# A six-sublayer decoder on one core: the order of matrix products in self-attention, the output projections in cross-attention, and eight-bit products with three weight tables

## The reference

```python
# 1 (cross-attention, 2, has the same skeleton with norms, rotation and a mask)
q = q * cq + rotate_half(q) * cq;  k = k * ck + rotate_half(k) * ck
attn = softmax(einsum('bhnd,bhmd->bhnm', q, k) * scale)
out  = einsum('bhnm,bhmd->bhnd', attn, v).reshape(b, n, H * HD) @ Wo
# 6
q1 = (input1 * scale).astype(float8_e4m3fn);  q2 = (input2 * scale1).astype(float8_e4m3fn)
out = (q1.astype(float32) / scale) @ (q2.astype(float32) / scale1)
```

## Time and profile before

| what | value |
|---|---|
| three executions | 2940.96, 2946.80, 2949.22 us, median 2946.8 us |
| the profiled execution | 2954.18 us, of which the span is 2952.3 us |
| TensorE busy | 2691.4 us, 91% of the span |
| VectorE busy | 1891.6 us, 64% |
| ScalarE busy | 1323.2 us, 45% |
| GpSimd busy | 1256.0 us, 43% |
| mean granted TensorE clock | 0.953 |

### The profile page before, as it was taken

One profiled execution on the slowest core, in us unless ns is written; L12 is line 12 of the kernel. 1 busy time (PEld: TensorE's weight loads), 2 busy tenths in 40 slices (PEclk: granted clock), 3 DMA queues, 4 the chain that ended last, 5 costly groups with the idle time before them and its releaser, 6 DMA issues. The chain is left out here.

```text
span 2952.3 us, 65025 instructions
## 1 busy us (share of the span) xinstructions
PE 2691.4 (91%) x23700; PEld 2323.1 (79%) x23700; DVE 1891.6 (64%) x4030; ACT 1323.2 (45%) x3154; POOL 1256.0 (43%) x1605
## 2 busy tenths in 40 slices
PE   6999999996699999999999979996999999699985
PEld 5888888886588888888888868885777777477773
DVE  5555555554677777777777744444777777366657
ACT  2222222222566666666666633332433333266656
POOL 3111111111476767676767601113455454334434
PEclk9999999998899999999999989997999999799985
DMA  4000000001100000000000020000000000000001
GB/s 141 7 7 4 7 7 4 6 4 41 58 6 5 4 5 4 5 4 5 4 5 4 2 74 0 0 0 28 13 8 11 7 11 0 26 30 28 28 4 58
DMA packets 42505, 49.12 MB, mean 17 GB/s; under 512 B 4032, under 2 KB 33600, under 8 KB 41920
## 3 DMA queue, kind: packets, MB, share of 16 engines
q1 hardware_dynamic: 42432, 48.16, 5.0%
HBM read 35.56 MB, written 4.19 MB: 13 GB/s over the span
## 5 line engine op out<-in xcount | busy, mean ns | idle before, releaser
L1033 ACT ACTIVATE b_probs<-bank,b_shift,b_q_scale 128x128 f32<-128x128 f32 x512 | 228.4, 462 | 0.6
L1092 POOL TENSOR_TENSOR b_rows<-b_rows,b_swapped 128x512 f32<-128x512 f32 x160 | 204.5, 1287 | 56.2 <-DVE b_swapped L878 56.2
L518 POOL TENSOR_TENSOR a_probs<-a_probs,a_rs 128x512 f32<-128x512 f32 x64 | 66.8, 1043 | 311.1 <-DVE a_rs L414 303.9
L1139 POOL TENSOR_TENSOR b_probs<-b_probs,b_rs 128x512 f32<-128x512 f32 x128 | 133.2, 1040 | 136.6 <-DVE b_rs L930 133.5
L2583 ACT ACTIVATE d_probs<-d_probs 128x512 f32<-128x512 f32 x128 | 78.9, 630 | 240.6 <-DVE d_probs L2482 238.7
L46 PE MATMUL bank<-a_xT,a_wq 128*128 128x256 f32 x512 | 153.7, 300 | 26.6 <-DVE a_xT L381 26.6
L1102 POOL TENSOR_TENSOR b_rms<-b_rms,sh_minus_half 128x8 f32<-128x8 f32 (+1 forms) x128 | 169.6, 1325 | 10.7
L886 DVE TENSOR_REDUCE b_ss<-b_squares 128x4 f32<-128x512 f32 x192 | 125.2, 680 | 73.7 <-ACT b_squares L1008 73.7
L134 POOL TENSOR_SCALAR sh_rstd<-sh_meanvar 128x2 f32<-128x2 f32 (+1 forms) x80 | 17.7, 222 | 326.0 <-DVE sh_meanvar L120 264.1
L46 PE MATMUL bank<-b_wo,b_oT 128*128 128x256 f32 x512 | 149.9, 293 | 1.4 <-DVE b_oT L852 1.4
L389 DVE TENSOR_TENSOR a_qT<-bank,a_cos 128x256 f32<-128x256 f32 x256 | 95.3, 419 | 85.2 <-PE bank L48 85.2
(11 more groups left out here) (350 smaller groups left out, 9060.0 us busy)
## 6 DMA issues: line engine op xcount, KB each, us to landing
a_xT_in<-in_xT SPq DMA_DIRECT2D x16, 256.0 KB, 2.6
sh_x<-in_x SPq DMA_DIRECT2D x1, 4096.0 KB, 25.0
b_ctx_in<-in_ctxT SPq DMA_DIRECT2D x32, 128.0 KB, 2.0
d_x_in<-sh_x SPq DMA_DIRECT2D x16, 256.0 KB, 2.3
e_x_in<-sh_x SPq DMA_DIRECT2D x16, 256.0 KB, 2.4
e_cT<-in_ctxT SPq DMA_DIRECT2D x32, 128.0 KB, 2.5
out<-sh_x SPq DMA_DIRECT2D x16, 256.0 KB, 2.1
a_qT<-in_L_attn_Wq SPq DMA_DIRECT2D x1, 2048.0 KB, 8.5
```

The source lines that it names most:

```text
L1033: op = act.activation(probs[:, g % 2, keys], bS[:, keys], ACT.Exp, bias=shift[:, g % 2, a:a + 1], scale=q_scale[:, g, a // 2, a % 2:a % 2 ...
L1092: pool.tensor_tensor(rows[:, unit, :], rows[:, unit, :], swapped[:, half, :], ALU.add).then_inc(added[unit], 1)
L1139: pool.tensor_tensor(pr, pr, rs[:, g % 2, :].unsqueeze(2).to_broadcast([128, R, 128]), ALU.mult).then_inc(probs_ready[g], 1)
```

## The change

In self-attention the attention of a group runs later against the projections and a third turn, `older`, comes in. TensorE's order becomes: s0 p2' q0 | s1 t0 q1 p3' | s2 t1 w0 q2 p0 | s3 t2 w1 q3 p1 | t3 w2 k w3 v v, where p2' and p3' belong to the turn before `before`. The islands are s0; s1 t0; s2 t1 w0; s3 t2 w1; t3 w2; w3: six. VectorE starts its turn with `low_o(older, 3)` and `low_x(now)`, takes the older turn's residual after group 1 and its statistics after group 2; ScalarE takes `take_o` ahead of the next `exponent` and copies the next rows at the end of its turn; GpSimd normalises after group 2. In cross-attention `project_out(old, 2)` moves to just ahead of `project_out(old, 3)`. In the eight-bit block `over`, `under` and `excess` go; `inner` is `coarse` clamped, and with w twice and w times minus two, fine·w + coarse·2w − inner·2w takes the place of fine·w + excess·w: twelve products in a turn.

```diff
@@ self-attention, TensorE
-            def turn(now, before):
+            def turn(now, before, older):
                 if before is not None:
                     scores(before, 0)
+                if older is not None:
+                    project_out(older, G - 2)
                 if now is not None:
                     pe.wait_ge(x_low, nth(now, 1, 1))
                     q_proj(now, 0)
-                for g in range(1, G):
+                if before is not None:
+                    scores(before, 1)
+                    transpose_probs(before, 0)
+                if now is not None:
+                    q_proj(now, 1)
+                if older is not None:
+                    project_out(older, G - 1)
+                for g in range(2, G):
                     if before is not None:
                         scores(before, g)
                         transpose_probs(before, g - 1)
+                        weigh_values(before, g - 2)
                     if now is not None:
                         q_proj(now, g)
                     if before is not None:
-                        weigh_values(before, g - 1)
-                        if g >= 2:
-                            project_out(before, g - 2)
+                        project_out(before, g - 2)
+                if before is not None:
+                    transpose_probs(before, G - 1)
+                    weigh_values(before, G - 2)
                 if now is not None:
                     k_proj(now)
                 if before is not None:
-                    transpose_probs(before, G - 1)
+                    weigh_values(before, G - 1)
                 if now is not None:
                     v_proj(now, 0)
-                if before is not None:
-                    weigh_values(before, G - 1)
-                if now is not None:
                     v_proj(now, 1)
-                if before is not None:
-                    project_out(before, G - 2)
-                    project_out(before, G - 1)
@@ self-attention, VectorE
-            def turn(now, before, after):
-                if before is not None:
-                    maximum(before, 0)
-                    total(before, 0)
+            def turn(now, before, older):
+                if older is not None:
+                    low_o(older, G - 1)
                 if now is not None:
-                    take_q(now, before, 0)
-                for g in range(1, G):
+                    low_x(now)
+                for g in range(G):
                     if before is not None:
                         maximum(before, g)
+                        if g >= 2:
+                            low_o(before, g - 2)
+                        total(before, g)
                     if now is not None:
                         take_q(now, before, g)
-                    if before is not None:
-                        total(before, g)
-                        low_o(before, g - 1)
+                    if older is not None and g == 1:
+                        residual(dve, sh, older, 2, [b[:, 0:D] for b in bY], y_ready, res_ready, norm_done)
+                    if older is not None and g == 2:
+                        row_stats(dve, sh, older, 2, res_ready, stats_ready, meanvar_ready)
+                if before is not None:
+                    low_o(before, G - 2)
                 if now is not None:
                     take_k(now, 0)
                     take_k(now, 1)
-                if before is not None:
-                    low_o(before, G - 1)
-                if after is not None:
-                    low_x(after)
-                if before is not None:
-                    residual_stats(dve, sh, before, 2, [b[:, 0:D] for b in bY], y_ready, res_ready, stats_ready, meanvar_ready, norm_done)
@@ self-attention, ScalarE
                 if before is not None:
                     exponent(before, 0)
-                for g in range(1, G):
-                    if before is not None:
+                    take_pT(before, 0)
+                    exponent(before, 1)
+                    for g in range(2, G):
                         take_pT(before, g - 1)
+                        take_o(before, g - 2)
                         exponent(before, g)
-                        take_o(before, g - 1)
-                if before is not None:
                     take_pT(before, G - 1)
+                    take_o(before, G - 2)
                     take_o(before, G - 1)
@@ cross-attention, TensorE
             def turn(new, mid, old):
                 project_vc(mid)
-                project_out(old, 2)
                 turn_unit(mid, Q + 2)
                 scores(mid, 1)
                 turn_unit(mid, Q + 3)
+                project_out(old, 2)
                 project_out(old, 3)
@@ eight-bit block
-                    for k, part in enumerate((fine, excess)):
+                    for k, (part, by) in enumerate(((fine, w), (coarse, w_twice), (inner, w_away))):
...
             def scale_rows(i):
                 act.wait_ge(turned, i + 1)
-                free(act, over_ready, i)
+                free(act, y_ready, i)
                 act.activation(coarse[:, i % 2, :], bT[i % 2][:, :], ACT.Copy, scale=halves[:, 0:1], saturate=False).then_inc(coarse_ready, 1)
+                free(act, fine_ready, i)
...
-                dve.tensor_scalar(over[:, i % 2, :], coarse[:, i % 2, :], TOP, 2.0, ALU.max, ALU.mult).then_inc(over_ready, 1)
+                dve.tensor_scalar(inner[:, i % 2, :], coarse[:, i % 2, :], TOP, -TOP, ALU.min, ALU.max, saturate=False).then_inc(inner_ready, 1)
```

More of the change, by code:

```diff
@@ L438, in turn @@
                     take_k(now, 1)
-                if before is not None:
-                    low_o(before, G - 1)
-                if after is not None:
-                    low_x(after)
-                if before is not None:
-                    residual_stats(dve, sh, before, 2, [b[:, 0:D] for b in bY], y_ready, res_ready, stats_ready, meanvar_ready, norm_done)
[L446 to L451, removed]
+            turn(0, None, None)
+            turn(1, 0, None)
+            with dve.Fori(2, n_turns) as i:
+                turn(i, i - 1, i - 2)
+            turn(None, n_turns - 1, n_turns - 2)
+            turn(None, None, n_turns - 1)
         @block.scalar
@@ L484, in take_o, with turn @@
                     act.copy(of_batch(0, g, b), bO[b][:, :].rearrange("p (r h q) -> p r h q", r=2, h=R)).then_inc(o_taken, 1)
[L486 to L488 removed]
+            def turn(now, before, following):
                 if before is not None:
                     exponent(before, 0)
[L491 to L492 removed]
+                    take_pT(before, 0)
+                    exponent(before, 1)
+                    for g in range(2, G):
                         take_pT(before, g - 1)
+                        take_o(before, g - 2)
                         exponent(before, g)
[L495 to L496 removed]
                     take_pT(before, G - 1)
+                    take_o(before, G - 2)
                     take_o(before, G - 1)
@@ L501, in turn @@
                     take_v(now, 1)
[L503 to L506, removed]
+                if following is not None:
+                    high_x(following)
+            high_x(0)
+            turn(0, None, 1)
+            with act.Fori(1, n_turns - 1) as i:
+                turn(i, i - 1, i + 1)
+            turn(n_turns - 1, n_turns - 2, None)
+            turn(None, n_turns - 1, None)
         @block.gpsimd
@@ L513, in _, with turn @@
             pool.wait_ge(x_loaded, 16)
-            with pool.Fori(0, n_turns) as i:
+            def turn(now, before):
                 for g in range(G):
[L516 to L519, removed]
+                    if now is not None:
+                        pool.wait_ge(rs_ready, nth(now, G, g + 1))
+                        pr = probs[:, g % 2, :].rearrange("p (a k) -> p a k", k=S)
+                        pool.tensor_tensor(pr, pr, rs[:, g % 2, :].unsqueeze(2).to_broadcast([128, 8, S]), ALU.mult).then_inc(probs_ready, 1)
+                    if before is not None and g == 2:
+                        normalise(pool, sh, before, 2, meanvar_ready, norm_step, norm_done)
+            turn(0, None)
+            with pool.Fori(1, n_turns) as i:
+                turn(i, i - 1)
+            turn(None, n_turns - 1)
 def cross_attention_block(nc, sh):
@@ L1413, in fp8_matmul_block @@
         unscale = sb("unscale", [128, 1])
-        edge = sb("edge", [128, 1])
         scaled = sb("scaled", [128, 3, 512])
         coarse = sb("coarse", [128, 3, 512], FP8)
-        over = sb("over", [128, 3, 512], BF16)
-        under = sb("under", [128, 3, 512], BF16)
+        inner = sb("inner", [128, 3, 512], FP8)
+        outer = sb("outer", [128, 512], BF16)
         fine = sb("fine", [128, 3, 512], FP8)
-        excess = sb("excess", [128, 3, 512], FP8)
         res = sb("res", [128, 2, 2, D])
@@ L1507, in _ @@
             scale_rows(0)
-            act.wait_ge(edge_set, 1)
-            below(0)
```

(12 more changed lines are left out.)

61 lines of the change are left out of this document (32 added, 29 removed).

## The result

| kernel | median of its runs, us | range | against before |
|---|---|---|---|
| before, four runs | 2948.0 | 2940.96 to 2951.93 | |
| changed, four runs | 2914.6 | 2911.31 to 2917.76 | 0.9889, 95% interval 0.9866 to 0.9912 |

The changed kernel is 33.5 us (1.1%) faster; the forecast was 2916 us, 30 us faster than the median of three. Its profiled execution took 2911.31 us (span 2909.5 us, mean granted clock 0.966).

The account below looks back on a forecast made before the run. TensorE bounds cross-attention, waits on GpSimd's probabilities in self-attention, and VectorE and ScalarE set the eight-bit turn. −47 + 24 − 7 = −30 us from the 2946.8 us median gives 2916 us; own range 2904 to 2928, 8-in-10 range 2892 to 2934.

Parts of the forecast that it names:

- Self-attention: Self-attention: both TensorE waits for the probabilities go, turn 42.6 to 39.9 us; −47 us in all.
- The tail: Last self-attention without projections: `take_o` before the exponent lies on its path; 3 us charged, bounds 0 and 8.
- The slack of 0.7 us: Self-attention, first transposes: probabilities ready at 7.3 us after s0, wanted at 8.0, so the wait goes with 0.7 to spare.
- the 6.0 us of the four slow turns: Self-attention: four turns of 44.1 us at the fallen 1.2 GHz clock; their 6.0 us counted within the 43.8 us gained.
- The joints: Self-attention: two islands fewer save 0.4 us, transposes running into w three times cost about 0.1 each; net 0.1 a turn.
- Cross-attention: Cross-attention: without p2 ahead, s1 waits 0.79 us for the exponent in each of 30 turns; +24 us, bounds 0 and 27.
- the release: Cross-attention: delay after the exponent before s1 may start, about 0.05 us within the 0.79 us wait.
- Rival A: Cross-attention: the stall doesn't come, the chain shortens or p2's cover was not needed; −54, 2893 us; chance 0.17.
- C: Slower: new idle time in cross-attention lowers TensorE's clock in every turn; +15, 2962 us; chance 0.07.
- Eight-bit block: Eight-bit block: turn 3.51 to 3.0 us for 15 turns, clock going up and down; −7 us, bounds −13.5 and +1.
- Rival D: Eight-bit block bound by TensorE at the low clock; +8 on the forecast, 2924 us; included in the forecast's 0.62.
- Rival B: Self-attention: a new wait of up to 1.4 us a turn at p1 or w3; 2936 us; chance 0.14.

Follow-up runs that it names:

- late_residual: Kernel before with only VectorE's residual and statistics and GpSimd's normalisation moved behind group 1 of the next turn, TensorE's order kept: 2917.21 us, one execution.
- seven_islands: Changed kernel with self-attention's transposes of group 0 put between the halves of group 1's query projection, one island more: 2912.98 us.
- eight_islands: Changed kernel with self-attention's values products of groups 0 and 1 moved between the halves of a query projection, eight islands for six: 2942.93 us, one execution.
- cross_only: Kernel before with only the change's cross-attention block: 2971.68 us, ratio 1.0086 to before.
- eight_only: Kernel before with only the change's eight-bit block: 2937.04 us, ratio 0.9961 to before.
- twelve_old: Kernel before with the eight-bit block's `excess` product taken twice, twelve products a turn, VectorE's and ScalarE's work kept: 2950.87 us, one execution.

## Why the prediction was right

**Self-attention, right (−47 predicted, −47.6 measured).** Turns 2 to 15: 39.9 us forecast, 39.89 to 39.90 measured. Turn 1: 41.7 − 6.4 = 35.3 forecast, 35.26 measured. The tail from the first scores without projections to the block's end took 36.5 us for 33.1 before, +3.4 where I charged 3: the projections of the last group wait for `low_o` (the lines of 4.0 and 1.5 us). late_residual shows the cause that I named, the residual and the normalisation ahead in the queues, and gives it about two thirds. The maxima start hardly earlier than before, though (1.85 us after s0; I had 2.2): `low_x` now stands where the residual was, and what makes the wait go is partly the absent normalisation (the multiplication ends 1.0 us earlier) and partly p2', which sends s1 2.8 us later (6.97 us after s0 for 4.14). The slack of 0.7 us that I gave it is 2.05. One term of the sum was luck: I took the 6.0 us of the four slow turns as a sure part of the gain. Three other traces with the same code had 3, 3 and 0 such turns. Against the one with none the block gains 40.5 us.

**The joints, right in the sum and wrong in the parts.** I priced an island at 0.2 us and the three touching transposes and values at 0.1 each, net −0.1 a turn. The remainder in the experiments is 0.13, but seven_islands gives 0.04 for an island of transposes and eight_islands nothing for one of values. Fewer islands is not what this change lives on: 2.57 of the 2.70 us a turn are waits that went, and the turns at the low clock come on top.

**Cross-attention, right (+24 predicted, +25.4 measured).** The wait is 0.67 to 0.8 us, 31 times, the chain from w2 kept its 10.1 us, and the turn is 29.95 to 29.98 us for the 29.9 forecast. I had taken 0.05 us for the release although showed 0.15; it is 0.15 here. A steady turn grew by 0.87 us where I had 0.79, which makes 2.4 us in 30 turns, and the block came out 1.4 over the forecast. That remainder is below what the block varies by: six kernels in which it has the code of before took 971.2 to 973.9 us for it. Rival A, that the stall stays away, is out; so is C: after the 30 waits in the steady turns the clock never fell, here or in the three other traces with this block (cross_only, eight_islands, seven_islands). The 1.8 us waits of the old self-attention were followed by the low clock in 10 of 56 turns (four traces with 14 each).

**Eight-bit block, mechanism right, size missed (−7 predicted, −11.0 measured, −11.9 in eight_only).** The step that failed reads "The clock will go up and down; I take 3.0". It did not go down: the clock was 1.00 from 2862 to 2902 us, the turn 2.61 us on average, the 2.6 that I had for 2.4 GHz. The sum by that price was −13.5. What it lost is at the start and the end: from the first transposes after the weights' preparation to the first residual are 3.8 us (2857.95 to 2861.76) where 3.0 were before, because twelve products instead of eight run there, still at 1.2 GHz; and the last turn before was a short one, 2.25 us, so only 14 turns could give the 0.9. Rival D had TensorE as the bound at 1.2 GHz. It did not come: after, the clock was not low, and before, the residuals stood 3.51 us apart in windows with a clock of 0.73 as in those of 0.50, so TensorE was not the bound there either. Whether twelve products at the low clock would be the bound of the new block stays open. Only the first turn of eight_only had them so for a part (2.1 us), and it took 2.90 us for 2.53. The Trainium skill (TensorE: Matmul & The Clock Gate, The HAM clock gate) has activity release the throttled state; the prediction set that aside for a clock that goes up and down. By that rule the turn would be 2.6 us, and the trace agrees: a clock of 1.00 and 2.61 us.

**Rival B**, a new wait at p1 or w3, stayed away in the changed kernel. eight_islands shows that it was near: 1.43 us later for the values, and p0 and p1 wait.

**The total.** The blocks sum to −33.2 us for the −30 forecast. The eight-bit block gained 4.0 us more than I said and self-attention 0.6 more, and cross-attention lost 1.4 more.

## What to carry to other kernels

Read where the queue of a helping engine stands when the busy engine stops: moving a residual, its statistics and a normalisation behind the next turn's urgent work gave 32.5 of 2950 us, one execution against one, with TensorE's own order untouched. Before products are moved off a place that looks arbitrary, ask what they cover: there the 1.4 us of p2 hid 0.7 us of an exponent, in each of 30 turns, and moving it cost 23 us for nothing in return. A change of several parts is worth running in parts: the change without one of them (2894.6 us) is faster than the change.

## What the runs showed that was not expected

- In the old eight-bit block the granted clock was the low one for 7 to 41 of 51.3 us, depending on the execution, and the steady turn was 3.51 to 3.52 us in all of them. With twelve products in the same 3.51 us (twelve_old, one execution) it did not fall, and they cost no time, since another engine is the bound.
- Idle times of 0.7 to 0.8 us every 30 us never lowered the clock in the steady turns of four traces. Those of 1.8 us every 42.6 us were followed by the low clock in 4, 3, 3 and 0 turns of 14, with the same code. A gain that hangs on such falls differs from one execution to the next.
- Islands of transposes and of values cost next to nothing: transposes start 0.12 us after an fp32r product and an added island of them costs 0.04 us, and an added island of values leaves the next products where they were. Scores start 0.21 us after one.
- The grouped attention, with the same code in all kernels, took from 325.5 to 333.1 us, and the quantised attention from 521.3 to 525.3 us. I have no cause for it. It is as large as some of the effects studied here, so a single execution's total says less than the length of the block in question.
